# Two score terms stacked on 96 rows, a two-product down projection, and work moved around in a cross-attention and expert kernel

## What is computed

```python
x = x + attn0(layernorm(x), ctx)     # 16 heads of 16; keys and values are ctx twice over, softmax over 2*77
x = x + ffn0(layernorm(x))           # hidden 1024; weight of an expert = mean of w_tok over its tokens
x = x + attn1(layernorm(x), ctx)     # one head of 256, with biases
x = x + ffn1(layernorm(x))           # hidden 256; each token's rows scaled by its score, plus a shared expert

# ffn0, expert e:
mask = sel.any(-1); w_tok = (topk_p * sel).sum(-1); mean_w = w_tok.sum() / max(mask.sum(), 1)
h = silu(xf @ gw.T) * (xf @ uw.T)
out = out + mask[:, None] * (h @ dw.T) * mean_w
```

## Time and profile before

| what | value |
|---|---|
| median of 3 runs | 741.76 us (740.7 to 746.59) |
| the profiled execution | 745.15 us |
| its span | 743.4 us (1.75 us lie around it) |
| instructions | 14230 |
| PE / PEld busy | 94% / 84% |
| DVE / ACT / POOL busy | 75% / 66% / 45% |

### The profile page before, as it was taken

One profiled execution on the slowest core, in us unless ns is written; L12 is line 12 of the kernel. 1 busy time (PEld: TensorE's weight loads), 2 busy tenths in 40 slices (PEclk: granted clock), 3 DMA queues, 4 the chain that ended last, 5 costly groups with the idle time before them and its releaser, 6 DMA issues.

```text
span 743.4 us, 14230 instructions
## 1 busy us (share of the span) xinstructions
PE 699.7 (94%) x4989; PEld 623.0 (84%) x4989; DVE 560.6 (75%) x992; ACT 490.1 (66%) x847; POOL 337.4 (45%) x333
## 2 busy tenths in 40 slices
PE   6899999989989999999999999999989879999994
PEld 6676777678989989998999899998978638999984
DVE  5776755686968868886868786886878978788847
ACT  3377777645647767776767676776746956787841
POOL 6558777502043323333233323332234657778840
PEclk9899999999999999999999999999999999999998
DMA  5000002267657868885877886795465264555439
GB/s 195 1 2 1 0 1 86 86 211 274 230 151 233 290 182 257 234 288 181 253 208 234 257 264 206 235 287 174 139 171 232 71 214 121 154 160 155 151 115 325
DMA packets 58264, 130.64 MB, mean 176 GB/s; under 512 B 6705, under 2 KB 30258, under 8 KB 58194
## 3 DMA queue, kind: packets, MB, share of 16 engines
q1 hardware_dynamic: 46674, 109.09, 43.1%
q0 software_dynamic: 11232, 20.46, 12.4%
q10 hardware_dynamic: 288, 0.19, 0.1%
HBM read 106.90 MB, written 22.81 MB: 174 GB/s over the span
## 4 chain that ended last, share of the span: by engine, by line
PE 70%; DVE 14%; POOL 5%; issue 4%; ACT 4%; DMA 2%; DVEq 0%; ACTq 0%; SPq 0%; POOLq 0%
PE ps L365 63%; DVE w_lo L1411 4%; POOL p_lo L749 2%; ACT w_hi L913 2%; PE ps L2570 2%; DVE h_lo L1411 1%; DVE x_all L2131 1%; PE ps L2806 1%; PE ps L2527 1%; DMA xm_d<-xnb 1%; PE ps L2279 1%; DVE hf L1853 1%; PE ps L2648 1%; DMA x_all<-in_x 1%; POOL xnb L862 1%
## 5 line engine op out<-in xcount | busy, mean ns | idle before, releaser
L1411 DVE TENSOR_TENSOR w_lo<-wr,w_hi 128x1024 fp32r<-128x1024 f32 x144 | 175.2, 1222 | 26.8 <-ACT w_hi L913 26.2
L804 POOL DMA_INDIRECT x_d<-ye,sca x39 | 74.1, 1900 | 247.6 <-ACT ye L1106 202.1
L913 ACT ACTIVATE w_hi<-wr 128x1024 fp32r<-128x1024 f32 x144 | 150.6, 1050 | 3.0 <-PE ps L365 2.2
L365 PE MATMUL ps<-xe_hi,w_lo 128*128 128x256 f32 x488 | 138.0, 283 | 0.0
L365 PE MATMUL ps<-xe_hi,w_hi 128*128 128x256 f32 x480 | 137.6, 287 | 0.2 <-DVE xe_lo L1411 0.2
L365 PE MATMUL ps<-xe_lo,w_hi 128*128 128x256 f32 x480 | 136.0, 283 | 0.0
L365 PE MATMUL ps<-w_hi,h_hi 128*128 128x256 f32 x312 | 91.7, 294 | 4.0 <-DVE h_lo L1411 2.2
L365 PEld LDWEIGHTS ps<-xe_hi,w_hi 128*128 128x128 f32 x480 | 92.2, 192 | 3.0 <-DVE xe_lo L1411 3.0
L365 PEld LDWEIGHTS ps<-xe_hi,w_lo 128*128 128x128 f32 x488 | 93.8, 192 | 0.1
L365 PEld LDWEIGHTS ps<-xe_lo,w_hi 128*128 128x128 f32 x480 | 92.2, 192 | 0.0
L365 PE MATMUL ps<-w_lo,h_hi 128*128 128x256 f32 x312 | 89.0, 285 | 0.0
(11 more groups left out here) (391 smaller groups left out, 1758.2 us busy)
## 6 DMA issues: line engine op xcount, KB each, us to landing
wr<-in_w SPq DMA_DIRECT2D x144, 512.0 KB, 4.5
dr<-in_w1d SPq DMA_DIRECT2D x24, 256.0 KB, 3.0
xn_d<-xnb SPq DMA_DIRECT2D x8, 512.0 KB, 3.7
raw<-in_w1gu SPq DMA_DIRECT2D x8, 512.0 KB, 9.2
x_d<-x_all SPq DMA_DIRECT2D x4, 512.0 KB, 4.6
x_all<-x_d SPq DMA_DIRECT2D x4, 512.0 KB, 4.3
xm_d<-xnb SPq DMA_DIRECT2D x4, 512.0 KB, 4.0
xnb<-y_d SPq DMA_DIRECT2D x4, 512.0 KB, 5.2
```

What stands on the lines that cost most here:

```text
L365: return nc.tensor.matmul(out, w, x, start=start, stop=stop, skip_group_check=True)
L804: pool.indirect_dma_start(dst, bass.IndirectOffsetOnAxis(ap=sca[n][:, col + half:col + half + 1], axis=0), ye[:, t % 2, half, :], None, co ...
L913: return s.activation(o, i, ACT.Copy)
L1411: return v.tensor_tensor(o, a, b, ALU.subtract)
```

## The change

- **Scores.** For the units u >= 1 two of the three products become one: k_hi's 48 rows of three heads lie twice in `ks` (96 rows), q_hi and q_lo of the same heads one under the other in `qs`, and one product of 96 rows gives both terms. The rows are put there by transfers from SBUF to SBUF on SP's queue: 16 for `ks`, two for each three heads of a unit for `qs` (three buffers in turn). For this, blocks are cut anew, two blocks to three heads (128 and 103 rows). The -1 rows move from k_hi to k_lo, so the maxima enter with the last product, and the wait for them stands there.
- **Start.** Four products that nothing reads stand ahead of the wait in `turn_rows(1)`, three ahead of that in `values(0)`.
- **Downs.** h_hi x w_hi and h_hi x w_lo become one product of 512 columns, whose two halves are added when they leave PSUM: ACT copies the one (`y0`, now counted by `dn_ok`), a new `y_lo0` on DVE adds the other (38 instructions). The last single keeps its three products.
- **Mean weights.** `sum_weights` and most of `mean_weights` (as `mean_tiles`) go to the end of router 0, the rest to the end of tile 0, with `y0(0)` and `y_lo0(0)`.
- **Router 1.** The cut is 12 and 4 tiles; DVE's order is changed, `raw_rows(3)` on ACT goes ahead of the exponents, and products that nothing reads fill two places.
- **`place`.** A reduction writes whole numbers at once, where a copy made them.

```diff
 def chosen(r, k):
-    cut = NT // 2 if r is r1 else NT - GT
+    cut = NT - GT
...
+def down_row(bank, hh, hl, wb, ws, start, stop):
+    mm(ps[:, bank, :].rearrange("p (k n) -> p k n", k=2), hh, w_hl[:, :, wb, ws], start, False)
+    return mm(ps[:, bank, 0:D], hl, w_hi[:, wb, ws], False, stop)
...
+def stack_queries(u):
+    sp.wait_ge(q_ls, parts_done(u))
+    if u == 2 * HG - 1:
+        sp.wait_ge(p_ls, 1)
+    if u > QRING:
+        sp.wait_ge(s_mm, FIRST[u - QRING + 1])
+    for i in range(trios(u)):
+        for k, part in enumerate((q_hi, q_lo)):
+            sp.dma_start(qs[u % QRING][trio_rows(k), i, :].bitcast(f32), part[trio_rows(i), slot_of(u), :].bitcast(f32)
+                         ).then_inc(w_in[2 + u % QRING], 16)
+sp.wait_ge(kv_hi, 1)
+for j in range(NW):
+    stack_keys(j)
+for u in range(1, NU):
+    stack_queries(u)
 with sp.Fori(0, NG) as g:          # SP: the stores xn_d <- xnb
...
 def y0(t):                         # ACT
                     s.activation(ye[:, t % 2, half, :], ps[:, 4 + half, 0:D], ACT.Copy,
-                                 scale=mw_t[:, SLOT[t]:SLOT[t] + 1]).then_inc(f0["y_ok"], 1)
+                                 scale=mw_t[:, SLOT[t]:SLOT[t] + 1]).then_inc(dn_ok, 1)
...
             raw_rows(2)            # ACT
             copy_logits1(2)
             normed_rows(1)
+            raw_rows(3)
             exponents(r1, 0)
-            raw_rows(3)
...
             tables(0, r0)          # DVE
+            link(v.tensor_copy(n_e[:, :], ps[:, 3, NT * E:(NT + 1) * E]))
+            sum_weights()
+            mean_tiles()
...
+            def y_lo0(t):          # DVE
+                for half in range(SPAN[t]):
+                    dve.wait_ge(dn_ok, NU + halves(t, half))
+                    v.scalar_tensor_tensor(ye[:, t % 2, half, :], ps[:, 4 + half, D:2 * D], mw_t[:, SLOT[t]:SLOT[t] + 1],
+                                           ye[:, t % 2, half, :], ALU.mult, ALU.add).then_inc(f0["y_ok"], 1)
...
                     if after and q == 0:   # DVE, pair0(t)
                         w0_lo(t, 2)
+                        y_lo0(t - 1)
...
                     w0_lo(t + 1, 3)
                     x_lo0(t + 1)
+                    y_lo0(t)
...
             residual1(1)           # DVE, router 1
+            statistics1(nb, "b", 1)
+            top_of1(3)
             keep_logits1(0)
-            top_of1(3)
-            statistics1(nb, "b", 1)
             residual1(2)
             keep_logits1(1)
-            dve.wait_ge(lg_ok, NG + 2)
-            exceed(r1, 0)
             statistics1(nb, "b", 2)
-            choose_first(r1, 0)
             residual1(3)
             keep_logits1(2)
+            dve.wait_ge(lg_ok, NG + 3)
+            exceed(r1, 0)
             statistics1(nb, "b", 3)
+            choose_first(r1, 0)
             choose_second(r1, 0)
...
             def turn_rows(g):      # PE
+                if g == 1:
+                    bank_free(pe, "x", KC + 1)
+                    idle_products(4, bank_of("x", KC + 1))
                 pe.wait_ge(na["xn"], g + 1)
...
             def scores(b):         # PE, units u >= 1
+                    if j == 0:
+                        pe.wait_ge(w_in[2 + u % QRING], stacked(u))
+                    mm(out, ks[:, bt, j, 0:w], qs[u % QRING][:, j // 2, :], True, False)
                 if j == 0:
                     pe.wait_ge(mt_ok, u + 1)
-                mm(out, k_hi[:, bt, cols], q_hi[:, slot_of(u), :], True, False)
-                mm(out, k_lo[:, bt, cols], q_hi[:, slot_of(u), :], False, False)
-                mm(out, k_hi[:, bt, cols], q_lo[:, slot_of(u), :], False, True).then_inc(s_mm, 1)
+                mm(out, k_lo[:, bt, cols], q_hi[:, slot_of(u), :], False, True).then_inc(s_mm, 1)
             def values(b):
+                if b == 0:
+                    pe.wait_ge(q_ls, 4)
+                    idle_products(3, 3)
                 pe.wait_ge(p_ls, b + 1)
```

More of the change, by code:

```diff
@@ L21 @@
 NW = -(-UW // P)
+TRIO = 3 * DH
+KS = 2 * TRIO
+START = [NKEY * 3 * (j // 2) + P * (j % 2) for j in range(NW)]
+SIZE = [(P, 3 * NKEY - P)[j % 2] for j in range(NW)]
+QRING = 3
 NU = NG * HG
@@ L413, in width, with trios, trio_rows, stacked @@
         def width(u, j):
-            return min(P, HEADS_OF[u] * NKEY - P * j)
+            return min(SIZE[j], HEADS_OF[u] * NKEY - START[j])
+        def trios(u):
+            return -(-BLOCKS_OF[u] // 2)
+        def trio_rows(i):
+            return slice(i * TRIO, (i + 1) * TRIO)
+        def stacked(u):
+            return 16 * 2 * sum(trios(i) for i in range(1, u + 1) if i % QRING == u % QRING)
+        def loaded(t, b):
+            first = {2: stacked(NU - 3), 3: stacked(NU - 2), 4: stacked(NU - 1), 5: 16 * 2 * NW}
+            return first.get(b, 0) + 16 * (t + 1)
         def group(t, g):
@@ L561, in _, with stack_keys @@
             sp.dma_start(bv[:, :], A["bv"]).then_inc(l1_in, 16)
+            def stack_keys(j):
+                at = slice(START[j], START[j] + SIZE[j])
+                for k in range(2):
+                    sp.dma_start(ks[trio_rows(k), :, j, 0:SIZE[j]].bitcast(f32), k_hi[trio_rows(j // 2), :, at].bitcast(f32)
+                                 ).then_inc(w_in[5], 16)
+            def stack_queries(u):
[13 more added lines that the diff above has]
+                stack_queries(u)
             with sp.Fori(0, NG) as g:
@@ L683, in _ @@
             link(g.memset(rowm[:, :, :], 1.0))
[L684 to L687, removed]
+            rowm4 = rowm[:, :, :].rearrange("p (a b) h -> p a b h", b=2)
+            link(g.affine_select(out=rowm4, in_=rowm4, compare_op=ALU.is_ge, fill=0.0, base=0,
+                                 pattern=[[3 * NKEY, 2], [P, 2], [-NKEY, HU]], channel_multiplier=1))
+            g.affine_select(out=rowm4, in_=rowm4, compare_op=ALU.is_ge, fill=0.0, base=NKEY - 1,
+                            pattern=[[-3 * NKEY, 2], [-P, 2], [NKEY, HU]], channel_multiplier=-1).then_inc(const_ok, 1)
             pool.wait_ge(const_ok, 3)
@@ L1458, in _ @@
             v.memset(zpad[:, :], 0.0)
-            v.memset(vraw[:, :, NW - 1, 0:UK], 0.0)
+            for j in range(1, NW, 2):
+                v.memset(vraw[:, :, j, 0:UK], 0.0)
             dve.wait_ge(const_ok, 2)
@@ L1754, in place @@
                                      slot[:, :, :].rearrange("p (o t) e -> p o t e", o=1).to_broadcast([P, 2, NT, E]), ALU.mult))
-                link(v.tensor_reduce(slot2[:, :, :], picked[:, :, :, :], AX.X, ALU.add))
-                link(v.tensor_copy(slot_i[:, :, :], slot2[:, :, :]))
+                with nc.allow_low_precision(reason="sums of whole numbers"):
+                    ins = v.tensor_reduce(slot_i[:, :, :], picked[:, :, :, :], AX.X, ALU.add)
+                link(ins)
                 v.tensor_scalar(sb_i[:, :, :], slot_i[:, :, :], P - 1, None, ALU.bitwise_and)
@@ L1888, in pair0 @@
                     w0_lo(t + 1, 5)
+                if t == 0:
+                    y_lo0(t)
             def places_last():
@@ L2542, in down @@
                 q, j = k // 2 if row is None else row, k % 2
-                out, hs = ps[:, 4 + half, 0:D], slice(half * P, (half + 1) * P)
+                hs = slice(half * P, (half + 1) * P)
                 ws = slice((k % 4) * D, (k % 4 + 1) * D)
-                mm(out, h_hi[:, q, j, hs], w_hi[:, wb, ws], start, False)
-                mm(out, h_hi[:, q, j, hs], w_lo[:, wb, ws], False, False)
-                return mm(out, h_lo[:, q, j, hs], w_hi[:, wb, ws], False, stop)
+                return down_row(4 + half, h_hi[:, q, j, hs], h_lo[:, q, j, hs], wb, ws, start, stop)
             def gate_up0(t, q):
@@ L2589, in pair0 @@
                         down_single(t - 1, 1)
-                    if t == 1 and q == 1:
-                        pe.wait_ge(ws_ok, 1)
-                        mm(ps[:, 6, 0:E], ones[:, :], wsum[:, :], True, True).then_inc(ws_mm, 1)
+                if t == 0:
+                    pe.wait_ge(ws_ok, 1)
+                    mm(ps[:, 6, 0:E], ones[:, :], wsum[:, :], True, True).then_inc(ws_mm, 1)
                 if t == 1:
```

70 lines of the change are left out of this document (41 added, 29 removed).

## The result

| | median | all executions shown |
|---|---|---|
| before | 741.76 us | 740.7 to 746.59 (3) |
| changed | 733.54 us | 733.08 to 733.82 (3) |

The ratio is 0.9864, with a 95% interval of 0.9822 to 0.9906: 1.4% faster. Measured a second time (e10), it was 733.28 against 740.48, ratio 0.9889 (0.9852 to 0.9926). The forecast was 728.5 in a range of 721 to 737: the sign is right, and 5 us of the gain did not come. The profiled executions are 745.15 before and 733.82 after, 11.3 apart, while the medians are 8.2 apart: of 67 executions of the kernel before, 16 took 744.9 us or more and the others at most 742.03, and the profiled one, at 745.15, stands with the 16.

What follows compares the result with a forecast made beforehand. PE, by far the busiest engine, was taken to bound the kernel. The terms sum to -14.8 us: 730.4 from the profiled 745.15, 727.0 from the median 741.76; the middle was taken as 728.5, range 721 to 737.

Steps and rivals of the forecast that it cites:

- The start: Start of the attention: idle products in two waits keep the clock up, gaining 3.3 us; 0 if they do not.
- The scores: First attention: 40 blocks lose one product each, -9.3 us of PE, 2.2 given back in waits: -7.1 us.
- Rival 2: First attention: held by the chains, not by PE's products; the whole 7.1 gone, 735.6 us; chance 0.10.
- Transfers: First score of a unit: waits for stacked rows taken as 0, range 0 to 2 us.
- Tile 1: Experts, tile 1: waits of 1.85 us for mean weights and ye go, half clock too; together -3.5 us.
- The downs: Experts' downs: 304 joined pairs save -3.65 us, partly lost behind singles, `y_lo0` in DVE's holes: -2.0 us.
- Router 1: Router 1: new DVE order delays keep_logits1(0) and the last store, gather follows, idle products cost 0: +1.3 us.
- place: `place`: one DVE instruction of the shortest kind less, -0.2 us.
- Rival 1: Start of the attention: the clock falls all the same, 731.8 us; chance 0.20.
- 4: Downs: joined products give nothing (+2.0) and `y_lo0` lands on DVE's chain (+3.4), 733.9 us; chance 0.07.

Runs made afterwards that it cites:

- e10: The changed kernel again, measured a second time: 733.28 us against 740.48 before.
- e11: The kernel before with the 4 + 3 idle products of the start and nothing else of the change: 740.93 us against 740.48 before.
- e6: The changed kernel with the mean weights and the result of tile 0 made late again, in tile 1: 740.25 us against 741.16 before.
- e4: The changed kernel with three products of 256 columns in the downs and no `y_lo0` on DVE: 735.85 us against 740.84 before.
- e7: The changed kernel with router 1's order and cut of before, idle products kept: 731.38 us against 741.16 before.
- e5: The changed kernel without router 1's 6 + 3 idle products and the wait for tables ahead of the three: 734.56 us against 741.16 before.
- e8: The changed kernel with the edits of e2 and e5 together: 731.89 us against 741.16 before.
- e3: The changed kernel without the 4 + 3 idle products at the start of the attention: 735.68 us against 740.84 before.
- e2: The changed kernel with `wide` copied by DVE right behind its reciprocals instead of by POOL: 732.47 us against 740.84 before.

## Why the prediction was right, and where it was not

- **The start (-3.3): one of two terms that failed.** The mechanism is right for the profiled execution, but its sum was taken off the median in full too. In the profiles the stage from values(0) to values(3) gained 3.9, of which 0.7 are three score products, so some 3.1 for the clock. The median of before does not hold this loss: with the idle products alone it is not lower (e11, 740.93 against 740.48). The spread of before's three runs, 740.7 to 746.59, was on the table and could have told it: two of them lay 3.4 and 4.4 us under the profile. The middle of 730.4 and 727.0 (it is 728.7, not 728.5) took only half of that back.
- **The scores (-7.1): the other, a term mis-sized.** The stack is worth 3.9. The growth of the wait for `wide` was forecast (2.2, measured 2.4). Left out were the chains that have a little slack and then none: from values(3) to values(43) PE's idle time grew from 3.9 to 7.9 us, that is by 4.1, of which 1.6 are waits for den, q_lo, a, lg and top_t. Of the 1.3 us that remain between 9.3 - 4.1 and 3.9, an estimate puts 1.0 down to the same waits: a product's record runs 0.40 us while the next could start after 0.23, so a wait costs some 0.17 more than its idle time, and there are six more of them (16 against 10). Rival 2, with the whole gain lost, is half true.
- **Transfers (0).** Right; 2.2 to 2.4 us against a lead of 9. The four issues of unit 1 took 3.0 us on SP, not 1 to 2.
- **Tile 1 (-3.5).** Right in kind; 4.3 in the profiles, 4.8 by e6. Against e11, whose trace has the same waits (0.3 and 1.5) and no lower clock there, it is 2.8: also here a part belongs to the executions in which the clock falls. The 4.3 and the 2.8 hold the 0.4 that the joined downs give in tiles 0 and 1; e6 keeps those, so its 4.8 does not.
- **The downs (-2.0).** Right in kind: 1.7 by e4, of which 1.3 in tiles 2 to 23, next to nothing in pairs behind a single, `y_lo0` hidden.
- **Router 1 (+1.3).** Size about right (1.6 by e7; 1.6 in the profiles from residual1(0) to the first down of layer 1), and so is its beginning, the late keep_logits1(0). But residual1(2) came 0.63 later and not 1.3, and the rest was made further on, by DVE's wait for PE and the choice for 12 tiles: that the sum fits is in part luck. The last two stores were issued 1.2 us later behind residual1(0), as forecast (598.25 - 564.93 and 586.96 - 552.47), and the gather moved with them: 41.03 us behind residual1(0), against 39.04 in e7 and 39.19 in e11. The profile of before, with 40.88, hides it, as its gather followed these stores by 7.56 us (changed 6.54, e7 6.03, e11 5.83). The end of the path is wrong: PE waits for gathered rows 0.17 us in before and not at all in the changed kernel and e7, so what counted was `ohb` on DVE, and with it PE. The idle products at nothing: so in e5's traced execution; e8's speaks against it.
- **place (-0.2).** Not tested alone. The stage between values(43) and tile 0 is 0.5 us shorter than in before's profile, 0.1 shorter than in e11's, so no run shows it apart.

With the terms as the runs without a lower clock in these stages show them (the downs in tiles 0 and 1 are in the 2.8), 0 - 3.9 - 2.8 - 1.3 + 1.6 - 0.2 = -6.6, against -8.2 and -7.2 between the medians. That the result lies inside the forecast's range owes much to its width: the nearest of the single times, 731.8, 733.9 and 735.6, are those of rivals 1, 4 and 2. Rival 1 has the amount (the start gives the median nothing) for another reason, 4 did not happen, 2 did in part.

## What to carry to other kernels

In this case a product taken off a busy TensorE was worth less than half its price, since short chains over other engines ran beside it: look, for each such chain, in which instruction's queue its middle step stands, and move that step before or together with the cut. Make the sum for the execution that the median shows; if the profiled one lies well above the median, ask first what it has that the others have not. And an order that helps the first half of a chain is judged by its last link.

## What the runs showed of the hardware

- The same waits do not always bring the clock down: 1.31 and 1.05 us of waiting at the start stood before half clock in the kernel before, 1.31 and 1.07 before full clock in e3. The waits of tile 1, 0.3 and 1.5 us, stood before half clock in before and before full clock in e11 (1.00 from 200 to 250 us).
- In e2, DVE's copy `wide` takes 0.29 to 0.30 us (256 columns) or 0.36 (384) when it does not begin beside a p_lo of POOL, and 0.88 to 1.37 when it does: it then ends 0.14 to 0.22 us behind that p_lo. DVE's copy and POOL's p_lo:

```profile
58.44 0.29 DVE L1586 COPY wide<-rec 128x256 f32<-128x256 f32 x1
...
86.23 0.88 DVE L1586 COPY wide<-rec 128x256 f32<-128x256 f32 x1
...
85.67 1.30 POOL L799 TENSOR_TENSOR p_lo<-p,p_hi 103x512 fp32r<-103x512 f32 x1 [0.25 <-ACT p_hi L1104]
```

The copy begins at 86.23, p_lo ends at 86.97, the copy at 87.11. The Trainium skill (SBUF — State Buffer, Who interferes with whom) says that a DVE instruction in a two-port mode, which copies can enter, and one of GpSimd take turns on a shared pair of ports, the first to issue holding it for its whole instruction; these rows agree, though no run shows the copy's mode. It may be one reason why moving `wide` to DVE gave 2.5 us and not more; how much of it, I did not measure.
